# Attention values held stationary in 32-column strips, with a new order of slots, in a graph transformer block

## The reference

```python
nx = layernorm(x) * ln1_g + ln1_b
q, k, v = (nx @ wq + bq), (nx @ wk + bk), (nx @ wv + bv)      # 8 heads of 32
bias = where(adj > 0, 0.1 * adj * adj, -inf)                  # the same for all heads
attn = softmax(q @ k.T / sqrt(32) + bias, axis=-1)            # 128 x 128 per head
x1 = x + (attn @ v) @ wo + bo
n2 = layernorm(x1) * ln2_g + ln2_b
out = x1 + gelu(n2 @ w1 + b1) @ w2 + b2                       # hidden width 1024
```

## Time and profile before

| what | value |
|---|---|
| median of 3 runs | 1781.69 us (1774.5 to 1782.0) |
| span of the profiled execution | 1774.1 us |
| PE busy | 1676.1 us, 94% |
| DVE busy | 1295.6 us, 73% |
| ACT busy | 899.1 us, 51% |
| POOL busy | 475.9 us, 27% |
| mean granted TensorE clock | 0.966 of full speed |

### The profile page before, as it was taken

The page is one execution under the profiler, slowest core; times in us unless marked ns, Lnnn a source line. Parts: engine busy times, 40 slices in busy tenths (PEclk is TensorE's granted clock), DMA queues, the critical chain, the costliest instruction groups (busy, mean ns, idle before and its releaser), DMA issues.

```text
span 1774.1 us, 32603 instructions
## 1 busy us (share of the span) xinstructions
PE 1676.1 (94%) x11836; PEld 1544.7 (87%) x11836; DVE 1295.6 (73%) x2387; ACT 899.1 (51%) x1416; POOL 475.9 (27%) x392
## 2 busy tenths in 40 slices
PE   5789999999999999999999999999999999999998
PEld 4678988898988898988898988898998898898887
DVE  3677767787777787767787777788767788777773
ACT  2335555445555445555454555545555554555542
POOL 2332123333123333123333113333213333212300
PEclk8679999999999999999999999999999999999999
DMA  6323434423443423443422443432443432343300
GB/s 184 72 52 86 102 81 91 91 64 76 101 94 77 100 57 73 101 95 77 101 66 64 101 95 80 98 72 64 95 98 77 98 83 57 90 98 80 78 13 24
DMA packets 85803, 146.43 MB, mean 83 GB/s; under 512 B 9488, under 2 KB 60944, under 8 KB 85776
## 3 DMA queue, kind: packets, MB, share of 16 engines
q1 hardware_dynamic: 85776, 146.06, 35.7%
HBM read 28.58 MB, written 16.78 MB: 26 GB/s over the span
## 4 chain that ended last, share of the span: by engine, by line
DVE 40%; SPq 21%; PE 11%; issue 11%; DMA 8%; ACT 5%; POOL 2%; DVEq 1%; ACTq 0%; POOLq 0%
SPq L327 21%; DMA stack<-hid_parts 8%; DVE xhat L909 7%; DVE rmax L823 6%; DVE soft L820 6%; DVE hid_parts L928 4%; PE work L374 3%; PE work L375 3%; PE work L376 3%; DVE st L879 2%; DVE xhat L898 2%; ACT hid L708 2%; DVE xt_lo L920 2%; POOL rstd L1022 2%; ACT hid_parts L719 2%
## 5 line engine op out<-in xcount | busy, mean ns | idle before, releaser
L940 DVE TENSOR_TENSOR hid_parts<-hid,hid_parts 128x512 fp32r<-128x512 f32 x256 | 174.4, 692 | 281.8 <-ACT hid_parts L719 281.8
L1019 POOL TENSOR_TENSOR ve<-mv,eps 128x4 f32<-128x4 f32 x64 | 12.9, 202 | 1246.6 <-DVE mv L884 949.3
L374 PE MATMUL work<-w_hi,hid_parts 128*128 128x256 f32 x1024 | 294.6, 288 | 0.0
L375 PE MATMUL work<-w_lo,hid_parts 128*128 128x256 f32 x1024 | 283.6, 277 | 0.0
L376 PE MATMUL work<-w_hi,hid_parts 128*128 128x256 f32 x1024 | 283.6, 277 | 0.0
L458 PEld LDWEIGHTS mixed<-vals,probt 128*128 128x128 f32 x2048 | 242.8, 194 | 2.3 <-ACT probt L643 2.2
L458 PE MATMUL mixed<-vals,probt 128*128 128x33 f32 x2048 | 243.0, 274 | 1.4 <-ACT probt L643 1.4
L653 ACT ACTIVATE soft<-soft 128x1024 f32<-128x1024 f32 x128 | 135.4, 1058 | 169.8 <-DVE soft L825 168.2
L708 ACT ACTIVATE hid<-work,b_col 128x512 f32<-128x512 f32 x256 | 174.8, 684 | 72.1 <-PE work L376 72.0
L374 PE MATMUL work<-nt_hi,w_hi 128*128 128x512 f32 x512 | 203.6, 398 | 3.4 <-ACT hid L708 1.9
L376 PE MATMUL work<-nt_hi,w_lo 128*128 128x512 f32 x512 | 200.5, 392 | 0.0
(11 more groups left out here) (95 smaller groups left out, 3544.7 us busy)
## 6 DMA issues: line engine op xcount, KB each, us to landing
stack<-hid_parts SPq DMA_DIRECT2D x384, 256.0 KB, 5.0
xin<-in_x SPq DMA_DIRECT2D x32, 512.0 KB, 3.8
out<-res SPq DMA_DIRECT2D x128, 128.0 KB, 1.7
adj_in<-in_adj SPq DMA_DIRECT2D x32, 256.0 KB, 4.0
res<-in_L_gnn_w SPq DMA_DIRECT2D x1, 1024.0 KB, 8.2
soft<-in_L_gnn_w SPq DMA_DIRECT2D x1, 1024.0 KB, 10.6
x<-in_L_gnn_wq SPq DMA_DIRECT2D x1, 256.0 KB, 4.0
x<-in_L_gnn_wk SPq DMA_DIRECT2D x1, 256.0 KB, 4.4
```

Source lines behind the costliest of these rows:

```text
L374: pe.matmul(o, lhs_hi, rhs_hi, start=first, stop=False)
L375: pe.matmul(o, lhs_hi, rhs_lo, start=False, stop=False)
L940: dve.tensor_tensor(hid_lo[:, m, :], hid[:, m % 3, :], hid_hi[:, m, :].bitcast(F32), ALU.subtract).then_inc(hid_lo_ready, 1)
```

## The change

- `mix`: the values are now the stationary operand, 32 columns per head, and the turned probabilities are the moving one, 128 columns. Head h goes to the strip of array columns and PSUM partitions `32*(h % 4)`, and to the half `h // 4` of the output columns. What comes out is already turned, so `turn_attn` is gone, and so is the column of ones.
- The row sums now come from the exponentials: ACT runs one per head, with the negated maximum as its bias and `accum_out` for the sum. The subtraction L825 is gone. `soft` is now two buffers by slot parity, worked on in place.
- `normalise` divides the probabilities (128x1024) by their sums before `turn`; `turn` waits for `normed` instead of `prob_ready`.
- `mixed` and `wout` are the two halves of one PSUM bank, `tail`, so `mix` waits for `x1_summed`. The freed bank makes three work banks (`BANKS = 3`).
- `values_copy` moves from ACT to DVE.
- The order of slots is new. PE now projects before `down`, runs one `down` in slot 0, two in slot 1 and one in slot 2, flips "xt" at the end of slot 0 and "nt" at the end of slot 1, and runs the four `query_key` blocks in one piece. `stats1` and `norm1` of the group n+2 run in slot 3. On POOL the bias of the edges comes ahead of the second `rstd`, and `result_start` waits for `nhat_ready`.

```diff
-UNITS = ([("down", 0, -2), ("down", 1, -2)]
-         + [("down", 2, -2), ("down", 3, -2)]
-         + [("qk", 0, 1), ("qk", 1, 1), ("qk", 2, 1), ("qk", 3, 1)]
+UNITS = ([("down", 0, -2)]
+         + [("down", 1, -2), ("down", 2, -2)]
+         + [("down", 3, -2), ("qk", 0, 1), ("qk", 1, 1), ("qk", 2, 1), ("qk", 3, 1)]
          + [("v", 0, 1), ("v", 1, 1)] + [("up", m, -1) for m in range(FC)])
+BANKS = 3
...
-        mixed = ps("mixed", [P, 512])
-        wout = ps("wout", [P, 512])
+        tail = ps("tail", [P, 512])
+        mixed, wout = tail[:, 0:D], tail[:, D:2 * D]
...
-                pe.wait_ge(prob_ready, step.graphs(s, 1))
+                pe.wait_ge(normed, step.graphs(s, 1))
...
-                for kind, slot, off in (("xt", 1, 1), ("nt", 2, -1)):
+                for kind, slot, off in (("xt", 0, 1), ("nt", 1, -1)):
                     if s == slot + 1 and step.has(off):
                         pe.wait_ge(taken[kind], step.count(off, DC, DC - 1))
...
                 if step.has_graph(s, 2):
-                    pe.wait_ge(at_taken, step.graphs(s, 2))
+                    pe.wait_ge(x1_summed, step.graphs(s, 2))
                 for h in range(H):
-                    mm = pe.matmul(mixed[:, h * VW:(h + 1) * VW], probt[:, h, :],
-                                   vals[:, par, b, h, :], start=True, stop=True)
+                    j, c = h % RPB, h // RPB
+                    mm = pe.matmul(mixed[j * HD:(j + 1) * HD, c * P:(c + 1) * P], vals[:, par, b, h, :],
+                                   probt[:, h, :], start=True, stop=True, tile_position=(0, j * HD))
                 mm.then_inc(mixed_full, 1)
...
-                act.activation(prob[:, :, :], sraw[:, :, :], ACT.Exp).then_inc(prob_ready, 1)
+                for h in heads:
+                    a = act.activation(soft[:, par, h, :], soft[:, par, h, :], ACT.Exp,
+                                       bias=nmax[:, par, h:h + 1], accum_out=rsum[:, par, h:h + 1])
...
+                dve.wait_ge(prob_ready, step.graphs(s, 0))
+                dve.reciprocal(rinv[:, par, :], rsum[:, par, :]).then_inc(sum_inverted, 1)
+                dve.wait_ge(sum_inverted, step.graphs(s, 0))
+                dve.tensor_tensor(soft[:, par, :, :], soft[:, par, :, :],
+                                  rinv[:, par, :].rearrange("p (h a) -> p h a", a=1).to_broadcast([P, H, P]),
+                                  ALU.mult).then_inc(normed, 1)
...
                 softmax(step, 0)
-                result(step, 0)
                 residual(step, 0)
+                result(step, 0)
+                attn_lo(step, 0)
                 normalise(step, 0)
...
-                pool.wait_ge(x1_summed, step.count(-1, GB, GB - 1))
+                pool.wait_ge(nhat_ready, step.count(-1, GB, GB - 1))
```

More of the change, by code:

```diff
@@ L450, in mix @@
                 b = (s - 1) % GB
+                if not step.steady and step.n == 0 and s == 1:
+                    pe.wait_ge(bo_added, 1)
                 pe.wait_ge(turned_taken, step.graphs(s, 1) * 2)
@@ L603, in body @@
                     up(step, m)
-                turn_attn(step, 3)
                 if not step.steady and step.n == -1:
@@ L672, in flip_hi @@
                        .then_inc(hi_taken[kind], 1)
-            def values_copy(step, half):
-                if not step.has(1):
-                    return
-                act.wait_ge(full["v"], step.count(1, 2, half))
-                if not step.steady and step.n == -1:
-                    act.wait_ge(ones_set, 1)
-                act.activation(
-                    vals[:, step.parity_of(1), half * 2:half * 2 + 2, :, 0:HD],
-                    work[:, bank_of("v", half), :].rearrange("p (b h d) -> p b h d", b=2, h=H),
-                    ACT.Copy).then_inc(taken["v"], 1)
             def query_key_copy(step, m):
@@ L749, in body @@
                 hidden_hi(step, FC - 1)
-                attn_hi(step, 3)
             steps(act, groups, body)
@@ L829, in normalise @@
             def normalise(step, s):
-                if not step.has_graph(s, 1):
+                if not step.has(0):
                     return
-                dve.wait_ge(mixed_full, step.graphs(s, 1))
-                heads = mixed[:, 0:H * VW].rearrange("p (h d) -> p h d", d=VW)
-                dve.reciprocal(rsum[:, :].rearrange("p (h a) -> p h a", a=1),
-                               heads[:, :, HD:VW]).then_inc(sum_inverted, 1)
-                dve.wait_ge(sum_inverted, step.graphs(s, 1))
@@ new lines, in normalise, with values_copy @@
+                dve.tensor_tensor(soft[:, par, :, :], soft[:, par, :, :],
+                                  rinv[:, par, :].rearrange("p (h a) -> p h a", a=1).to_broadcast([P, H, P]),
+                                  ALU.mult).then_inc(normed, 1)
+            def values_copy(step, half):
+                if not step.has(1):
+                    return
+                dve.wait_ge(full["v"], step.count(1, 2, half))
+                dve.tensor_copy(
+                    vals[:, step.parity_of(1), half * 2:half * 2 + 2, :, :],
+                    work[:, bank_of("v", half), :].rearrange("p (b h d) -> p b h d", b=2, h=H)
+                    ).then_inc(taken["v"], 1)
@@ L1000, in _ @@
             dve.wait_ge(g1_ready, 1)
+            before = Step(-2, -1, 0, groups, False)
+            stats1(before)
+            norm1(before)
+            setup()
             steps(dve, groups, body)
```

211 lines of the change are left out of this document (92 added, 119 removed).

## The result

The changed kernel takes 1865.95 us (median, 1863.16 to 1867.14), the kernel before 1781.85 us beside it. The ratio is 1.0485, 95% interval 1.0461 to 1.0509: it is slower, and 14 us above the forecast of 1852. The profiled execution took 1866.29 us for a span of 1864.5.

What follows compares the result with a forecast made beforehand. PE bounds all but the stack-transfer stretch; DVE and ACT take over before slot 1's turn. Stretches 19.1 + 12.4 + 11.15 + 11.05 = 53.7 us, plus 1.46 for the clock, 55.16 a step: 1852 us, range 1785 to 1908.

Steps and rivals of the forecast that it cites:

- Stretch A: From the end of the last query/key block to the next scores: unchanged at 19.1 us, set by the stack transfers.
- Stretch B: From the scores to slot 1's turn: 12.4 us, 1.5 more than before, as DVE and ACT take over from PE.
- The start of the exponentials: Slot 0's exponentials on ACT would start 6.47 us after the scores, against 8.06 before.
- E: The eight exponentials on ACT in one slot, sum output included: 2.6 us, bounds 2.2 and 3.8.
- The fourth rival: The sum output costs 0.2 us for each exponential, making the eight take 3.8: 1905 us. Chance 0.07.
- The last piece: After slot 0's exponentials: at_hi, at_lo, reciprocal, division, two xt differences and waking PE, 3.3 us.
- mix: Sixteen instructions on PE, only neighbours of different heads overlapping: 1.1 us, bounds 0.43 and 1.9, against 1.70 before.
- the fifth rival: All four strips of mix run side by side, 0.43 us: 1818 us. Chance 0.07.
- C: From slot 1's turn to slot 2's turn: 11.15 us, 0.4 more than before.
- D: From slot 2's turn to the end of the last query/key block: 11.05 us against 11.41, three banks removing a 1.21 us wait.
- The clock: One fall of PE's granted clock in every step, near slot 1, costing 1.46 us.
- the second rival: The same chain, but the clock stays up between scores and slot 1's turn: 1807 us. Chance 0.18.

Runs made afterwards that it cites:

- e1_filled: The changed kernel with 40 unused matmuls of 256 columns added on PE in slot 0, 14 after the first down, 26 after the flips: 1849.3 us, ratio 1.0376.
- e2_down_back: The changed kernel with the second down, and its result on DVE, moved back from slot 1 to slot 0: 1826.61 us, ratio 1.0274.
- e6_edges_back: The changed kernel with POOL's edges back behind the start of the result: 1844.86 us, ratio 1.0365.
- e3_no_sum: The changed kernel without the sum output of the exponentials, row sums taken as 1: 1823.94 us, ratio 1.0264.
- e8_dense: The changed kernel with slot 0's xt flips ahead of mix, two downs moved one slot ahead, slot 2's first query/key block ahead of mix: 1819.17 us.
- e11_dense_all: e8_dense plus an early one-column exponential to load the table, POOL's edges back, and slot 1's division ahead of norm2: 1739.05 us, ratio 0.9781.
- e12_dense_early: e8_dense plus only an early one-column exponential on ACT, ahead of flip_hi, to load the table: 1724.21 us, ratio 0.97.

## Why the prediction was right, point by point

**Direction and mechanism: right.** The division and the exponentials stand between the scores and the next turn with less of PE's work over them than they take, and PE, which set B before, waits for DVE. The chain of rows that I named is the chain of the trace: maximum, eight exponentials, `at_hi`, `at_lo`, reciprocal, division, two differences. e1_filled and e2_down_back put 2.8 us and more of PE's work into B without lengthening it (13.4 in both, in e1_filled where no fall lies in it).

**Stretch A, 19.1: right** (19.12). PE's shorter work went into a longer wait for the transfers, 1.0 us instead of 0.5, less than the 1.4 that I gave as a sign.

**Stretch B, 12.4: 1.0 too low** (13.43). Three terms. The start of the exponentials was 6.47 and is 6.93 (817.11 to 824.04), because I let `hidden_lo` keep its length beside POOL's edges; I wrote "Hidden" for `norm1` and looked for its cost in A, where the slower `hidden_lo` shows as the later softmax of B. e6_edges_back gives 0.42 for it. E was 2.6 and is 3.1. Half of that is the sum output, which I set at 0.05, "since the sum adds no columns"; it is an instruction of its own and costs 0.08, 0.65 instead of 0.4 for eight. The other half is the exponentials themselves, 2.45 in e3_no_sum where I had 2.2. The fourth rival had the right mechanism at more than twice the price. The last piece was 3.3 and is 3.44 (827.14 to 830.58):

```profile
827.53 0.42 DVE L826 TENSOR_TENSOR at_lo<-tail,at_hi 128x256 fp32r<-128x256 f32 x1 [2.41 <-ACT at_hi L647]
827.87 0.19 DVE L805 RECIPROCAL rinv<-rsum 128x8 f32<-128x8 f32 x1
828.10 1.22 DVE L807 TENSOR_TENSOR soft<-soft,rinv 128x1024 f32<-128x1024 f32 x1
829.24 1.28 DVE L899 TENSOR_TENSOR xt_lo<-turned,xt_hi 128x512 fp32r<-128x512 f32 x2
```

**mix, 1.1: too high** (0.57). The step that failed is the sentence that the two instructions of a head and the neighbours limit the overlap. It is a third of the old time; the fifth rival, 0.43, was nearer. The trace agrees with the rule that I cited from the Trainium skill (TensorEngine Tiling (Array Packing), Key Properties), that tiles run in parallel. The 4x that the Trainium skill gives at most for 32 columns (the same page, Theoretical Speedup) would be, as an estimate, 0.43 here, so about 0.14 remain for everything else, the change of tiling mode among it.

**C, 11.15: 10.76 without a fall** (from e1_filled), and D, 11.05: 10.55. D is lower by the 0.5 of `mix`; the third bank did remove the wait in it. C was misadded: the terms that I listed, 4.37, `mix` 1.1, 2.82, 1.2 and 2.18 for the copies and the difference, make 11.67. In e1_filled `mix` took 0.57, the flips 0.8 and what follows them 1.9, so C came 0.9 below its terms, and only 0.4 below my sum by luck. The full-clock step is 19.12 + 13.43 + 10.76 + 10.55 = 53.9, where I had 53.7: two errors of 1 us each that cancel.

**The clock, 1.46: too low.** The measured step is 55.94, so it costs 2.1. I was right that it falls in every step and near slot 1, and took the price of one 3.4 us fall of before; here the fall lasts 6.8 or 10.2 us in 11 of the 28 steps. The kernel before loses 52.94 - 52.18 = 0.76 by the same count. Of the 3.0 us a step by which the kernel is slower, about 1.7 are therefore the chain and 1.3 the clock. The wait of up to 3.6 us in the changed kernel is longer than I had assumed, but length alone does not explain the falls: in e8_dense PE never waits longer than 2.4 us and still runs 6.7 us a step at half clock. That goes against the rule that I weighed, which gave the second rival, no fall in B (the Trainium skill, TensorE: Matmul & The Clock Gate, Why this matters for your kernels).

**The medians.** I added 7.6 us to the span, the distance between the median of before and a profiled execution that was among its fastest. Here the median is 1.5 above the span. That alone hid 6 of the 20 us by which the span was underrated (1844 against 1864.5), so the 14 us of the result are in part luck.

Of the signs that I named, PE's share, the wait at the turn (3.5 us), the wait of `mix` (1.8), no wait in D, the clock once a step and E between 2.2 and 3.8 came as written. The step is 0.4 above the upper end of 55.5, and the wait for the transfers is below the 1.4 named.

## What to carry to other kernels

Before an operation is moved onto the path from one product to the next, lay out which of PE's own work still lies over it; the change saved PE 107 us and lost 90. The same operations gain 55 with two `down` in each of the first two slots, the "xt" flips ahead of `mix`, and the table loaded early. A wait of PE is worth more than its length when the falls of the clock go with it: removing a 1.3 us load from a path in each of 31 steps brought 95 us, not 40, where the falls went, and 33 where they stayed. And look what else an operation will now run beside: moving one division and POOL's edges took 0.8 us a step back in another slot (e11_dense_all). On ACT, count what the name of an operation hides: the read of the sum behind each instruction, and the table that is loaded at the first exponential after a Gelu, which should fall where ACT waits anyway.

## What the runs showed of the hardware

- `accum_out` on an activation is a second instruction, ACTIVATION_READ_ACCUMULATOR, 188 ns, of which 80 to 90 ns show in a row of eight.
- Float32 products with 32 stationary columns in four strips run four abreast, 16 instructions in 0.57 us instead of 1.70, in either order of the heads.
- ACT's table load, 1283 ns twice a step, happens where the first instruction of the new function stands in the program, and does not wait for that instruction's data: in the changed kernel it ran ahead of the wait for the maximum (`soft` waits 0.95 us more after it). One exponential of a single column, 0.20 us, is enough to place it.
- POOL's edges beside DVE made a 512-column difference of two operands 814 ns instead of 688. Four normalising instructions with one tensor operand took 4.12 us beside POOL, 1.38 without. A division of 1024 columns took 2.05 us beside the edges, 3.15 beside the start of the result, and 1.22 without.
- The granted clock fell to the lower level in every step of the kernels in which PE waits 2.4 to 4.2 us at slot 1's turn. In e12_dense_early, with 0.94 there and 1.64 at slot 2's turn, it fell in 2 of 28 steps; in e11_dense_all, with 1.9 ahead of the scores, in 7 of 28; in the kernel before, whose longest wait is 1.2 us, in every second step. Filling the waits of B in e1_filled left falls in 10 of 28 steps, each at a wait of 2.7 to 4.6 us ahead of the scores. What exactly decides whether it falls stays open.
